# Graph kernel on one Trainium2 core: the table of edge counts kept column by column

## What is computed

```python
msg_in = jnp.concatenate([x[row], x[col], edge_attr], axis=-1)
h = msg_in @ W + b
# h is normalised over its 128 numbers, times gamma, plus beta
msg = jax.nn.relu(h)
out = jax.ops.segment_sum(msg, row, num_segments=x.shape[0])
...
x = _layernorm(x + out, axis=-1)
```

## Time and profile before

| | |
|---|---|
| median of 3 runs | 1759.11 us (1758.96 to 1759.6) |
| the profiled execution | 1758.61 us, its span 1756.8 us |
| mean granted clock of TensorE | 0.812 of full |
| busy: PE, DVE, ACT, POOL | 1201.1, 949.3, 711.4, 771.9 us |
| L784, the fold | 16 matmuls, once, at 95.43 us |
| L1423, the copies to `by_col` | 13, from 59.0 to 93.1 us |

### The profile page before, as it was taken

How to read it: one execution, slowest core, us unless ns; L and a number is a source line. 1 busy time by engine, 2 the same in 40 slices (tenths; PEclk the granted TensorE clock), 3 DMA queues, 4 the chain that set the end, 5 groups by cost and what they waited for, 6 DMA issues and landing times.

```text
span 1756.8 us, 36181 instructions
## 1 busy us (share of the span) xinstructions
PE 1201.1 (68%) x9913; PEld 1049.7 (60%) x9914; DVE 949.3 (54%) x2787; ACT 711.4 (40%) x2814; POOL 771.9 (44%) x810
## 2 busy tenths in 40 slices
PE   6598776666766666766666666667666667656775
PEld 5455666655666556666566666566555656655662
DVE  7623355545555445554455555455455455538997
ACT  3223343433434333443334333344344344335766
POOL 0335544455444455444554444554445554450003
PEclk9767777878878788787888778788888777878998
DMA  7665455344443444444444443444444444312322
GB/s 213 170 129 137 127 154 147 111 127 131 129 115 116 124 131 129 120 115 125 126 130 130 115 128 113 131 130 127 112 120 126 131 128 128 111 54 80 92 65 73
DMA packets 192458, 215.22 MB, mean 123 GB/s; under 512 B 51350, under 2 KB 141802, under 8 KB 192272
## 3 DMA queue, kind: packets, MB, share of 16 engines
q1 hardware_dynamic: 166236, 160.39, 35.1%
q0 software_dynamic: 25088, 51.83, 8.5%
q10 hardware_dynamic: 948, 0.79, 0.2%
HBM read 144.85 MB, written 68.06 MB: 121 GB/s over the span
## 4 chain that ended last, share of the span: by engine, by line
PE 39%; another core or an unknown queue 24%; issue 18%; ACT 10%; DVE 6%; DMA 2%; DVEq 1%; SPq 0%; ACTq 0%
PE bank L962 11%; PE bank L940 7%; PE bank L916 7%; ACT late L1183 5%; PE bank L856 5%; PE bank L930 3%; PE bank L969 2%; ACT turn L1145 1%; DVE late L1580 1%; PE bank L846 1%; DMA tabB<-room 1%; PE bank L844 1%; ACT late L1189 1%; DVEq L493 1%
## 5 line engine op out<-in xcount | busy, mean ns | idle before, releaser
L683 POOL DMA_INDIRECT rows<-p,pos_idx x784 | 756.0, 964 | 825.3 <-ACT p L1149 535.0
L1145 ACT COPY turn<-bank 128x512 f32<-128x512 f32 x196 | 115.0, 587 | 688.0 <-remote 523.3
L962 PE MATMUL bank<-wc,turn 128*128 128x128 f32 x1552 | 297.2, 351 | 66.9 <-ACT turn L1145 59.9
L940 PE MATMUL bank<-room 128*128 x2592 | 246.4, 250 | 106.6 <-issue 61.4
L962 PEld LDWEIGHTS bank<-wc,turn 128*128 128x128 f32 x1552 | 257.4, 251 | 88.1 <-ACT turn L1145 79.3
L940 PEld LDWEIGHTS bank<-room 128*128 128x128 bf16 x2592 | 204.3, 115 | 128.0 <-issue 117.6
L1183 ACT ACTIVATE late<-room 128x128 f32<-128x128 f32 x864 | 256.4, 303 | 2.7 <-issue 1.3
L916 PE MATMUL bank<-late 128*128 128x129 f32 x1472 | 230.3, 299 | 33.9 <-issue 31.4
L1580 DVE SCALAR_TENSOR_TENSOR late<-room,late,floor 128x128 f32<-128x128 f32 x864 | 248.1, 349 | 0.4 <-issue 0.3
L916 PEld LDWEIGHTS bank<-late 128*128 128x128 f32 x1472 | 207.5, 214 | 26.4 <-issue 26.0
L1175 ACT COPY room<-bank 128x512 bf16<-128x512 bf16 x216 | 127.0, 588 | 223.9 <-remote 128.8
(11 more groups left out here) (240 smaller groups left out, 1256.1 us busy)
## 6 DMA issues: line engine op xcount, KB each, us to landing
p<-in_edge_attr_dram SPq DMA_DIRECT2D x98, 512.0 KB
room<-rows SPq DMA_DIRECT2D x256, 129.0 KB
near_bc<-near SPq DMA_DIRECT2D x98, 256.0 KB
late<-rows SPq DMA_DIRECT2D x176, 129.0 KB
rows<-p,pos_idx POOLq DMA_INDIRECT x784
win<-tabB SPq DMA_DIRECT2D x196, 31.5 KB
rows<-fill SPq DMA_DIRECT2D x24, 193.5 KB
tabB<-room SPq DMA_DIRECT2D x12, 384.0 KB, 3.8
```

What stands on the lines that cost most here:

```text
L683: nc.gpsimd.indirect_dma_start(rows_ap, bass.IndirectOffsetOnAxis(pos_idx[:, k, j:j + 1], 0), stage[:, k, j, :], None).then_inc(st_free[k] ...
L940: mm = pe.matmul(bank[A_BANK + b2][:, jj * D:(jj + 1) * D], selT[b2][:, jj * P:(jj + 1) * P], tabA[:, bass.ds(at[jj // UJ], 1), part, :], ...
L962: pe.matmul(bank[H_BANK + h][:, t * D:(t + 1) * D], eT[h][:, t * P:(t + 1) * P], wc[:, 2, :], start=(t == 0), stop=False, skip_group_check ...
L1145: nc.scalar.copy(eT[h], bank[E_BANK][:]).then_inc(eT_ready, 1)
```

## The change

The table `by_col` is laid out with the column outermost: for one partition first the 392 numbers of column 0, then those of column 1, and so on. The copy DVE makes (L1423) now writes runs of 32 numbers side by side, 16 runs, and reads its PSUM bank with a step of 16 numbers of 4 bytes. The moving operand of each product of the fold is one run of 392 numbers. Counts of instructions, their order, the waits and the results stay as they are.

```diff
-        by_col = room[0:DU * DC, SUMS + TABA:SUMS + TABA + C * DV // 2].bitcast(BF16).rearrange("p (t v c) -> p t v c", v=DV, c=DC)
+        by_col = room[0:DU * DC, SUMS + TABA:SUMS + TABA + C * DV // 2].bitcast(BF16).rearrange("p (c r) -> p c r", c=DC)
...
                     mm = pe.matmul(bank[O_BANK][0:2 * DU, 0:C // DC * DV], fold[:, c, :, :].rearrange("p o u -> p (o u)"),
-                                   by_col[:, :, :, c], start=(c == 0), stop=(c == DC - 1))
+                                   by_col[:, c, :], start=(c == 0), stop=(c == DC - 1))
...
-                nc.vector.tensor_copy(by_col[:, 4 * i:4 * i + n, :, :].rearrange("p t v c -> p (t v c)"),
-                                      bank[COUNT_BANK[i % 2]][0:DM, 0:n * DV * DC]).then_inc(s_ccr, 1)
+                nc.vector.tensor_copy(by_col[:, :, 4 * i * DV:(4 * i + n) * DV],
+                                      bank[COUNT_BANK[i % 2]][0:DM, 0:n * DV * DC].rearrange("p (r c) -> p c r", c=DC)).then_inc(s_ccr, 1)
```

## The result

The changed kernel takes 1746.71 us (median of 5 runs, 1744.87 to 1753.15) beside 1758.96 us for the kernel before on the same chip (5 runs, 1756.9 to 1759.6). The ratio is 0.995, its 95% interval 0.9927 to 0.9973: by the medians 12.25 us faster, by the ratio 8.8 us, between 4.7 and 12.8. The profiled executions stand closer together: 1753.15 us (span 1751.3) after and 1758.61 us (span 1756.8) before, 5.5 us. So the profile shown here is that of the slowest of the five runs, and part of the 12 us is not in it. The mean clock was 0.814 in it, and 0.817 to 0.822 in the other four.

The account below looks back on a forecast made before the run. It took a chain of hand-overs, with PE the bound from 95.4 to 110.8 us; 7.6 us gained at ACT's copy, copies and clock at nothing, took 1758.61 to 1751.0, plus 0.5 for the median: 1751.5, range 1744 to 1760.

Parts of the forecast that it names:

- The fold: PE's 16 products with adjacent operands: about 3.0 us in place of 11.3, 8.4 us less at full clock.
- What comes last: After the fold, `a_mult` ends at 100.5; ACT's copy waits for group 2's scatters until 103.3, gaining 7.6 us.
- The copies to `by_col`: DVE's 13 copies: 0.07 us more each by L1430, 0.8 us in all, covered by waits, so costed at nothing.
- The far end, L1378's price: DVE's copies to `by_col`, priced by a line jumping in SBUF: 0.68 us more each, 8.1 us in all.
- the rival on the slower side: DVE's copies stall PE at L1378's price: 8.1 us lost, 4.5 us slower overall, 1763.6 us; chance 0.12.
- The hold of group 3: Rival: signals blocked until 118.5, behind group 3's scatters, take back 3.9 of 7.6 us; 1755 to 1759, chance 0.19.
- The clock: PE's half clock after the fold: more gain possible, but left out of the sum because group 3's hold follows.
- The price of the clock in the rival's sum: Steps 8 and 9: two thirds of some 16 us of half-clock work at full speed, 4.5 to 5 us less.
- the rival with the clock on top: No hold in group 3, PE at full clock from about 108: 1746.5 to 1747 us; below 1748, chance 0.17.
- the sign that the prediction had set itself: Forecast wrong if the time is outside 1748 to 1755 though L784 fell to 0.17 to 0.18 us between starts.

Follow-up runs that it names:

- e3: Changed kernel with six throwaway products for each operand step of 1, 2, 4, 8 and 16 numbers put ahead of the fold; one execution, 1743.13 us.
- e1: Changed kernel with the fold run twice, 32 products in place of 16, on a chip with holds; 1731.76 us, ratio 0.9957 to the kernel before.
- e6: Changed kernel with the fold run twice, on a chip without holds; 1234.74 us, ratio 0.9925 to the kernel before.
- a2: Changed kernel again, no edit, on a chip without holds; 1231.81 us, ratio 0.9904 to the kernel before.
- a1: Changed kernel again, no edit, on another chip with holds; 1733.87 us, ratio 0.9966 to the kernel before.
- e4: Changed kernel with the fill_pad writes moved to groups 5 to 14, from groups 1 to 13; 1735.2 us, ratio 0.9978 to the kernel before.
- e2: Changed kernel with the fold run four times, 64 products, on a chip with holds; 1736.73 us, ratio 0.9984 to the kernel before.
- e7: Changed kernel with the fold run four times, on a chip without holds; 1236.76 us, ratio 0.9941 to the kernel before.
- e5: Kernel before the change with the fill_pad writes moved to groups 5 to 14, from groups 1 to 13; 1744.08 us, ratio 1.0036.
- b1: Kernel before the change again, no edit, on a chip without holds; 1244.37 us, ratio 1.0006.

## Why the prediction was right, and where its sum was off

*The fold: right.* 3.0 us forecast, 2.86 measured, at full clock. (The clock had been full for 4.6 of the old fold's 11.4 us, rather more than the third that the prediction names.) That the step of the operand sets the pace was read off equal durations over both clocks; e3 shows it directly.

*What comes last: right.* `a_mult` ran at full clock and ended at 100.3 (forecast 100.5), ACT was held until 103.24 (forecast 103.3), and 110.88 - 103.24 = 7.6 us is the gain at that copy, as forecast. The distance from group 2's first scatter to this copy repeats on chips A and B: 11.8 and 11.4 us with the change, 19.5 without. The test by e1 is that 2.7 us more in the fold moved this copy by 0.8 us with holds; without them (e6 against a2, both from group 2's first scatter) it moved by 3.2 us, 11.1 against 7.9.

*The copies to `by_col`: right to cost them at nothing.* They cost nothing even per copy: 682 ns with a step of 64 bytes in PSUM, beside 683. The 0.07 us taken from L1430 is not there, so L1430's 1.15 ns a number need not come from its step. The far end, L1378's price, is on the SBUF side and did not carry over to PSUM. The rule of the Trainium skill, "Vector Engine (DVE) Microarchitecture Reference", section 5.2, would have made it 1.44 us (the prediction's estimate by that page); the trace does not bear it out for a read of PSUM. So the rival on the slower side had no ground. The page states the rule of SBUF alone.

*The hold of group 3: a rival, and it came, in the profiled execution.* The sum had 7.6 us carried to the end. In the profiled execution a second hold stood at 118.17, where the rival had put it (118.5), and it took 4.0 us, which the rival had priced at 3.9. That the price agrees to a tenth is luck: in a1, the same kernel, the copy of group 3 waited 3.70 us in place of 6.60, and in e1 not at all. The reason given for it (full DMA engines) does not hold: e4 had a hold in group 2 at a share of 0.46, and e1 had none at this copy at 0.85. When a group's scatters hold a copy and when they let it through is not known. Its 1755 to 1759 us did not come either; the profiled execution took 1753.15 us.

*The clock: the term that was mis-sized.* The sum had it at nothing, since another hold would pull the clock down. It did, to 13.7 us of half clock from 110.7, but 27.3 us of it had been there before, and what remained was worth more than nothing: 3.1 us on chip A (e2) and 5.8 us on chip D (e7), both with a fold as long as the old one. These two figures are rather high for the change itself, since the longer dense fold kept the clock up for longer than the short one (half clock from the fold's start to group 5's first scatter: 8.2 us in e2, 19.2 in a1). What is left for the length is 2.9 us of the 6.0 on chip A and 4.2 us of 10.0 on D. So the forecast of 7.6 us, all of it length, was near the total with a split that these two chips do not bear out: part of the length is swallowed later, and the clock gives some of it back. The price of the clock in the rival's sum was a little low by its own words: two thirds of 16 us at twice the speed are 5.3 us less, not 4.5 to 5. The split of A and D is no rule. On chip B the kernel before with late pads had 20.8 us of half clock over the same stretch and the changed one 17.3, hardly a difference, and their medians are still 8.9 us apart; why is open.

*The total.* 1746.71 against 1751.5: the forecast was 4.8 us too high. The time is inside the range, but 1.3 us under the forecast's own 1748 to 1755, where the rival with the clock on top stood. By the sign that the prediction had set itself (outside 1748 to 1755 though L784 fell as said) the forecast failed. The term that e2 and e7 point to is the clock, put at nothing; that it was the clock in the first chip's own runs is not shown. The overlap of both chips' intervals, 4.7 to 8.4 us, holds the 7.6 of the forecast. What made the first chip's five runs 12 us faster by the medians, when its profiled one was 5.5 and chip A's eleven were 6.0, is open. The clocks of the other four (0.817 to 0.822 beside 0.814) might point to the clock, but in a1 time and clock did not go together, and no trace of those runs exists. With runs of the changed kernel up to 13 us apart, a median of five can be off by some us by chance.

## What to carry to other kernels

Keep the moving operand of a matmul adjacent, or at most every second bf16, and put the rearranging into the copy that VectorE makes from PSUM anyway: the read with a step of 64 bytes was free, the matmul's read with a step of 32 bytes cost four times the product. Before counting the saved time, look for what releases the next hand-over; 8.6 us off PE were 7.6 us there, and one group later 4 us in one execution and 7 in another of the same kernel. Slow matmuls can cost twice: their own length, and the clock of the dense work behind them (3.1 and 5.8 us in the two comparisons here).

## What the runs showed that had not been expected

- The same kernel took 1759, 1740 or 1244 us. In the slower two, ACT waits "remote" until 1.4 to 2.2 us after POOL's last indirect scatter of the group, in 94 of the 98 groups of the profiled execution after the change, and 524 us in sum before the copies of the edges alone; in the third no copy of ACT's waits so. One run of 12 on a chip of the 1244 kind took 1740.91 us. It is not the kernel, not the share of the DMA engines (e4, e1), and not the scatters' length. What it is stays open: nothing on record ends the wait, and no run here switched it on or off.
- That one run had a granted clock of 1.0 over its whole length and took 1740.91 us, beside 1240 to 1249 us at 0.93 to 0.96 for the others on that chip. No trace of it exists. If it had holds, as its time suggests, the holds don't cost their 500 us by way of the clock.
- In the strided fold the clock fell to half 4.0 to 4.6 us after its start, though PE had been busy without a gap, on both kinds of chip (before, e5, b1). It stayed there for 27.3 us in two of the three, and for 13.7 us in e5, the same fold with the pads late. Dense products of the same total length (e2, e7) left it at full.
- The pace of a matmul by the step of its operand goes 1, 1, 2, 4, 4 for steps of 1, 2, 4, 8 and 16 bf16 numbers at full clock; at 16 the clock no longer matters; 4 and 8 were measured at full clock alone.
